# A recurrent megakernel: the fill turned by seven steps, gates of block 1 by DMA, low-rank products ahead of the base products

## The reference, cut to what matters

```python
# layer 0: shared MLP + 2 of 8 experts, gates from a sigmoid router
s = sigmoid(x_flat @ router_w.T + t_bias);  idx = top_k(s + router_bias, 2)
combine = sum(gates[:, :, None] * one_hot(idx, 8), axis=1)
H = gelu(einsum('nd,ehd->enh', x_flat, rw1));  O = einsum('enh,edh->end', H, rw2)
x = x + (silu(x @ sw1.T) * (x @ sw3.T) @ sw2.T + einsum('end,ne->nd', O, combine)) / 3
# layer 1: the sum and difference tree rebuilds v * gate
x = x + (x + x * sigmoid(silu(c @ W1.T + b1) @ W2.T + b2))
# layer 2: a1, b1, a2, b2 come from the condition (RANK = 8)
u = x a2;  mid = gelu(x @ base_down + u b2);  v = mid b1
x = x + (x + mid @ base_up.T + v a1)
# layer 3, for t in range(512):
Z = sigmoid(xz + H @ Whz.T + bhz);  R = sigmoid(xr + H @ Whr.T + bhr)
Ht = tanh(xh + (R * H) @ Whh.T + bhh);  H = Z * H + (1 - Z) * Ht;  Y = H @ Whq.T + bhq
x = x + Ys
```

## Time and profile before

| what | us |
|---|---|
| median of 3 runs (lowest, highest) | 1163.85 (1162.99, 1165.19) |
| the profiled execution, its own time | 1164.93 |
| its span | 1163.3 |
| TensorE busy | 1151.1 (99%) |
| VectorE busy | 893.1 (77%) |
| ScalarE busy | 509.4 (44%) |
| first scan of the state begins / last begins | 62.9 / 1157.9 |

### The profile page before, as it was taken

How to read it: one execution, slowest core, us unless ns; L and a number is a source line. 1 busy time by engine, 2 the same in 40 slices (tenths; PEclk the granted TensorE clock), 3 DMA queues, 4 the chain that set the end, 5 groups by cost and what they waited for, 6 DMA issues and landing times.

```text
span 1163.3 us, 56694 instructions
## 1 busy us (share of the span) xinstructions
PE 1151.1 (99%) x23581; PEld 1104.0 (95%) x23581; DVE 893.1 (77%) x5908; ACT 509.4 (44%) x2417; POOL 86.8 (7%) x163
## 2 busy tenths in 40 slices
PE   9899999999999999999999999999999999999998
PEld 8699999999999999999999999999999999999975
DVE  5568887777878777887777788777778777778765
ACT  1444444444444444444444444444444444444433
POOL 1200000000000000000000000000000000000000
PEclk9999999999999999999999999999999999999999
DMA  9511001111101110100111110011111001011000
GB/s 345 220 26 31 17 17 31 31 31 31 31 4 31 31 31 30 31 25 10 30 31 30 31 31 12 22 31 31 30 31 26 9 30 31 30 31 26 3 7 11
DMA packets 43297, 44.20 MB, mean 38 GB/s; under 512 B 7432, under 2 KB 39696, under 8 KB 41760
## 3 DMA queue, kind: packets, MB, share of 16 engines
q1 hardware_dynamic: 40720, 39.70, 11.3%
q10 hardware_dynamic: 2256, 0.82, 0.3%
q0 software_dynamic: 64, 0.07, 0.0%
HBM read 35.89 MB, written 4.69 MB: 35 GB/s over the span
## 4 chain that ended last, share of the span: by engine, by line
PE 96%; DVE 2%; DMA 1%; issue 1%; ACT 0%; SPq 0%; ACTq 0%; POOL 0%; DVEq 0%
PE bank L422 48%; PE gate_rh L422 28%; PE gate_z L422 12%; PE gate_rh L425 7%; DMA xt<-in_xT 1%; DVE state L1293 0%; ACT hin L885 0%; DVE peak L1367 0%; DVE upeaks L1364 0%; DVE upeaks L1375 0%; DVE upeaks L1373 0%; DVE hist L1295 0%; DVE state L1297 0%; DVE upeaks L1356 0%; DVE ge L1139 0%
## 5 line engine op out<-in xcount | busy, mean ns | idle before, releaser
L422 PE MATMUL gate_rh<-state,whp 128*128 128x8 f16 x5122 | 247.0, 166 | 0.0
L885 ACT ACTIVATE rg<-gate_rh 128x16 f32<-128x16 f32 x512 | 93.7, 183 | 337.7 <-PE gate_rh L422 337.7
L422 PEld LDWEIGHTS gate_rh<-state,whp 128*128 128x128 f16 x5122 | 199.3, 96 | 24.9 <-issue 8.0
L422 PE MATMUL bank<-x,upw 128*128 128x128 f16 x2880 | 218.3, 218 | 0.0
L422 PE MATMUL gate_rh<-rhp,whp 128*128 128x8 f16 x5120 | 216.6, 166 | 0.0
L539 PEld LDWEIGHTS <-whp 128*128 128x128 f16 x2046 | 201.6, 99 | 4.5
L422 PEld LDWEIGHTS gate_rh<-rhp,whp 128*128 128x128 f16 x5120 | 181.2, 96 | 7.4 <-issue 0.5
L885 ACT ACTIVATE zg<-zsum 128x16 f32<-128x16 f32 x512 | 110.6, 216 | 166.6 <-DVE zsum L1282 166.6
L422 PE MATMUL gate_z<-state,whp 128*128 128x16 f16 x4096 | 179.7, 176 | 0.0
L425 PE MATMUL gate_rh<-state,whp 128*128 128x8 f16 x1022 | 170.9, 167 | 1.8 <-DVE state L1293 0.6
L425 PE MATMUL gate_rh<-rhp,whp 128*128 128x8 f16 x1024 | 171.4, 167 | 0.3 <-DVE rhp L1277 0.3
(11 more groups left out here) (202 smaller groups left out, 1929.8 us busy)
## 6 DMA issues: line engine op xcount, KB each, us to landing
gates<-gates_t SPq DMA_DIRECT2D x30, 512.0 KB, 5.3
aw<-in_aw SPq DMA_DIRECT2D x4, 2048.0 KB, 23.3
out<-osb SPq DMA_DIRECT2D x32, 128.0 KB, 2.7
xt<-in_xT SPq DMA_DIRECT2D x30, 128.0 KB, 4.4
rw<-in_rw SPq DMA_DIRECT2D x2, 1024.0 KB, 10.2
sw<-in_sw SPq DMA_DIRECT2D x3, 512.0 KB, 6.7
wh<-in_wh SPq DMA_DIRECT2D x3, 256.0 KB, 11.8
wx<-in_wx SPq DMA_DIRECT2D x3, 256.0 KB, 20.0
```

The costliest lines, as they stand in the source:

```text
L422: return pe.matmul(o, w, x, start=start, stop=stop, skip_group_check=True)
L885: return act.activation(o, i, f, **kw)
```

## The change

The fill is turned by two more steps (TURN 5 to 7), so a fill round begins in real step 7 of its block, and must have its projections ready two fill steps sooner. For that the fill steps 4 to 10 are arranged anew: the low-rank product of g2 comes ahead of the base product of layer 2, `up_low` and `finish_l2` come a step sooner, the projections stand in fill steps 6 to 8 and not in 7 to 9, `sum_x` stands in step 7 and not in 8, the scores in step 6 (hole A) and not in 5 (hole B), `add_router_bias` in `early` of step 7 and not of 6, and the experts' gelu and gating one or two steps later. `exp_scores`, `fit_sum` and `fit_back` stay as they were.

In the set-up, the gates of block 1 go through DRAM on ScalarE's queue (a write of 16 KB, a broadcast read of 512 KB) and not through 8 calls on TensorE, the last experts of block 1 (4 chunks of 2 calls) move into the first two steps, `sum_x` for block 2 stands behind two of the chunks and reads its sum from the copy of x that was loaded early, the bits of two banks are set sooner, and each of the three wx loads has a semaphore of its own.

```diff
-TURN = 5
+TURN = 7
...
             def spread_gates(r):
-                sp.wait_ge(rows_ready, r - 1)
-                if r > 2:
-                    sp.wait_ge(gates_in, 16 * (r - 2))
+                sp.wait_ge(rows_ready, r)
+                sp.wait_ge(gates_in, 16 * (r - 1))
                 sp.dma_start(gates_dram, comb_rows[:]).then_inc(comb_out, 16)
-                sp.wait_ge(comb_out, 16 * (r - 1))
-                if r > 2:
-                    sp.wait_ge(ge47_done, r)
-                    sp.wait_ge(ge03_done, r)
+                sp.wait_ge(comb_out, 16 * r)
+                sp.wait_ge(ge47_done, r)
+                sp.wait_ge(ge03_done, r)
                 sp.dma_start(gates[:], gates_dram.rearrange("(q e) j -> q e j", q=QUADS)[:, 0:EXPERTS]
                              .partition_broadcast(P)).then_inc(gates_in, 16)
...
+            def experts_03_chunk(m, par, c):
+                if c == 0:
+                    pe.wait_ge(sa_done, count(m, 1))
+                    pe.wait_ge(xpow_done, 1)
+                up_chunks(A1, rw1, par, range(c, c + 1), ex03_done, c == 3)
+
             def between_z_h(m, par, s, has_y, has_l23, has_l0, has_router):
...
                 if has_y and s == 0:
                     y_products(later(m, -1), q, 0, 9)
                 if has_l0:
-                    for at, lo, hi in ((1, 11, 20), (7, 64, 73), (10, 77, 86)):
-                        if s == at:
-                            x_products(m2, par, lo, hi)
+                    if m[1] < 0 and s in (9, 10):
+                        experts_03_chunk(m2, par, 2 * (s - 9))
+                    if m[1] >= 0:
+                        for at, lo, hi in ((1, 11, 20), (9, 52, 61), (10, 75, 84)):
+                            if s == at:
+                                x_products(m2, par, lo, hi)
...
                     if s == 4:
-                        up_base(m1, (0,))
+                        pe.wait_ge(g2_done, count(m1, 1))
+                        low_in_rank(g2, start=True)
                     if s == 5:
-                        low_in_rank(g2, v_done)
-                    if s == 6:
-                        up_low(m1)
+                        pe.wait_ge(vm_done, count(m1, 1))
+                        up_base(m1, (1,))
+                    if s == 7:
+                        project_part(q, 3, 5)
                     if s == 8:
-                        project_part(q, 3, 5)
-                    if s == 9:
                         project_part(q, 8, 10)
-                if m[1] == BLOCKS - 2 and s in (1, 7, 10) or m[1] == BLOCKS - 2 and s > 10 or m[1] == BLOCKS - 1 and s > 0:
+                if has_router and s == 6:
+                    scores(later(m, 3), 1 - par).then_inc(scores_done, 1)
+                if m[1] == BLOCKS - 2 and (s in (1, 6) or s > 8) or m[1] == BLOCKS - 1 and s > 0:
                     keep_busy(2)
 
             def between_steps(m, par, s, has_y, has_l23, has_l0, has_router):
...
-                    for at, lo, hi in ((0, 0, 11), (1, 20, 24), (2, 24, 28), (3, 28, 42), (4, 42, 46), (5, 46, 50),
-                                       (6, 50, 64), (9, 73, 77), (10, 86, 96)):
-                        if s == at:
-                            x_products(m2, par, lo, hi)
+                    if m[1] < 0 and s in (9, 10):
+                        experts_03_chunk(m2, par, 2 * (s - 9) + 1)
+                    if m[1] >= 0:
+                        for at, lo, hi in ((0, 0, 11), (1, 20, 24), (2, 24, 28), (3, 28, 42), (4, 42, 46), (5, 46, 48),
+                                           (8, 48, 52), (9, 61, 75), (10, 84, 96)):
+                            if s == at:
+                                x_products(m2, par, lo, hi)
...
-                if has_router and s == 5:
-                    scores(later(m, 3), 1 - par)
                 if has_l23:
                     if s == 1:
                         mid_base(m1, (0,))
                     if s == 2:
-                        low_in_rank(x2, u_done)
+                        low_in_rank(x2).then_inc(u_done, 1)
                     if s == 4:
-                        up_base(m1, (1,))
-                    if s == 7:
+                        up_base(m1, (0,)).then_inc(v_done, 1)
+                    if s == 5:
+                        up_low(m1)
+                    if s == 6:
                         pe.wait_ge(x3_done, count(m1, 1))
                         pe.wait_ge(seeded, 2 * (m1[1] + 1))
                         project_part(q, 0, 3)
-                    if s == 8:
+                    if s == 7:
                         if has_router:
                             sum_x(later(m, 3))
                         project_part(q, 5, 8)
-                    if s == 9:
+                    if s == 8:
                         project_part(q, 10, 12)
...
-            sum_x((0, 2), 1)
             for k in range(KC):
                 i = mm(gate_rh[0][:, k * P:(k + 1) * P], low[:, 0, k * P:(k + 1) * P], ident[:], True, True)
             i.then_inc(lowT_pe, 1)
             pe.wait_ge(l2_in, 16)
             mid_base(m0)
+            pe.wait_ge(score_in, 3)
+            up_chunks(E47, rw1, 1, range(4, 5), ex47_done, False)
             pe.wait_ge(ready_dve, 4)
-            low_in_rank(x2, u_done)
-            spread(m1)
+            low_in_rank(x2).then_inc(u_done, 1)
+            set_bits(gate_rh[0]).then_inc(bits_set, 1)
+            up_chunks(E47, rw1, 1, range(5, 6), ex47_done, False)
+            pe.wait_ge(sa_done, 2)
+            sum_x((0, 2), 1)
             adapt(1, 0)
-            pe.wait_ge(score_in, 3)
-            up_chunks(E47, rw1, 1, range(4, 6), ex47_done, False)
+            up_chunks(E47, rw1, 1, range(6, 8), ex47_done, True)
             pe.wait_ge(low_dve, 2)
             mid_low(m0)
-            up_chunks(E47, rw1, 1, range(6, 8), ex47_done, True)
-            pe.wait_ge(xpow_done, 1)
-            set_bits(gate_rh[0]).then_inc(bits_set, 1)
+            adapt(1, 1)
             pe.wait_ge(g2_done, 1)
             pe.wait_ge(gs_done, 2)
             for k in range(KC):
                 i = mm(A3[:, 0:TOK], a2b1[:, k], g2[:, k], k == 0, k == KC - 1)
             i.then_inc(v_done, 1)
-            pe.wait_ge(sa_done, 2)
-            up_chunks(A1, rw1, 1, range(0, 2), ex03_done, False)
-            adapt(1, 1)
             pe.wait_ge(up_in, 16)
-            up_base(m0)
+            up_base(m0, start=True)
             first_reset_gate()
             pe.wait_ge(low_dve, 3)
             up_low(m0)
             set_bits(gate_z[0]).then_inc(bits_set, 1)
-            up_chunks(A1, rw1, 1, range(2, 4), ex03_done, True)
...
-                    if s == 8:
+                    if s == 10:
...
+            act.wait_ge(rows_ready, 1)
+            act.dma_start(gates_dram, comb_rows[:]).then_inc(comb_out, 16)
...
+            act.wait_ge(comb_out, 16)
+            act.dma_start(gates[:], gates_dram.rearrange("(q e) j -> q e j", q=QUADS)[:, 0:EXPERTS]
+                          .partition_broadcast(P)).then_inc(gates_in, 16)
-            sum_sizes((0, 2), 0)
+            act.wait_ge(ahead_in, 16)
+            sum_sizes((0, 2), xahead[:])
...
+                    if s == 5:
+                        keep_own(m1, vm, 1, v_done, vm_done)
                     if s == 6:
-                        keep_own(m1, vm, 1, v_done, vm_done)
-                    if s == 7:
                         finish_l2(m1, q)
...
-                        silu_a1_part(m2, s - 4)
+                    if s in (4, 7):
+                        silu_a1_part(m2, s // 7)
                     if s in (8, 9):
                         times_a3_part(m2, par, s - 8)
-                    if s in (10, 11):
-                        times_gate_part(m2, 1, s - 10, pe47_done, ge47_done)
-                if has_l0 and s in (12, 13):
-                    part = times_gate_part if m[1] >= 0 else times_spread_part
-                    part(m2, 0, s - 12, pe03_done, ge03_done)
+                if has_l0 and s in (11, 12):
+                    times_gate_part(m2, 1, s - 11, pe47_done, ge47_done)
+                if has_l0 and s in (13, 14):
+                    times_gate_part(m2, 0, s - 13, pe03_done, ge03_done)
                 if has_router:
-                    if s == 6:
-                        add_router_bias(m3)
-                    if s == 9:
-                        fit_x(m3)
-                    if s == 10:
-                        fit_x_end(m3)
-                    for at, k in ((11, 4), (14, 8), (14, 9), (15, 11), (15, 12)):
+                    if m[1] >= 0:
+                        if s == 7:
+                            add_router_bias(m3)
+                        if s == 9:
+                            fit_x(m3)
+                        if s == 10:
+                            fit_x_end(m3)
+                    for at, k in ((9, 1), (10, 3), (11, 5), (14, 9), (15, 11), (15, 12)):
                         if s == at:
                             gate_op(m3, k)
-                    if s == 14:
```

(60 more changed lines are left out.)

37 lines of the change are left out of this document (13 added, 24 removed).

## The result

Median over the runs that stood beside each other: 1163.42 us before, 1213.27 us after (1210.57 to 1218.68), a ratio of 1.043 with a 95% interval of 1.040 to 1.047. The forecast was 1197, its range ended at 1209. The profiled execution of the changed kernel took 1210.57 us, so the profile shows the cheapest of its runs; its span is 1208.8, which is 45.5 more than the 1163.3 before.

What follows compares the result with a forecast made beforehand. TensorE, without idle time in a step, was taken to bound the kernel; the time hung on the first scan and waits in the fill. -8.6 + 0 + 38.0 + 3.5 = +32.9 us gave 1197 us, range 1187 to 1209.

Steps and rivals of the forecast that it cites:

- the rival that had one: Each round's new TensorE wait also halves the clock afterwards: 51 us more, 1248 us; chance 6%.
- Part 3: Fill step 7: TensorE waits at `sum_x` for GpSimd's exponential and floor, 1.31 us a round, 38.0 us in 29 rounds.
- Part 1: Set-up: shorter wait, `spread`, experts and low clock bring the first scan 8.6 us sooner, bounds 5 and 10.5.
- some 0.4 of it hid x3: Set-up: of 1.8 us for block 1's last experts, some 0.4 hid x3, leaving 1.4 us gained.
- Part 2: Fill's turn and layer-2 order: covered by the recurrence's own matmuls, 0 us, bounds -1 and +3.
- Part 4: VectorE in fill step 15: `rest_x` makes `rhp` 0.12 us late a round, 3.5 us, bounds 0 and 7.
- The rival "no wait": Fill step 7: the sum reaches TensorE in time, so the set-up decides: 1159 us; chance 5%.

Runs made afterwards that it cites:

- e2: The changed kernel with five 512-column matmuls on zeros ahead of the waiting `sum_x` in fill step 7, so TensorE works through the wait; 1193.05 us.
- e1: The changed kernel with the floor of the sum issued ahead of the exponential in GpSimd's list of a round; 1158.23 us.
- e5: e1 with the first half of `rest_x` moved on VectorE from fill step 15 to step 0 of the next round; 1154.71 us.

## Why the prediction was wrong, step by step

- **The failed step: the clock set at nothing in the likeliest case.** The sum had no term for it; the rival that had one got 6%. It weighed one row, 4.12 us idle and then half rate, and called a stretch a third as long harmless because dense work stands on both sides. In fact 1.08 us was enough in half of the rounds: 17 us in the profiled execution, 20 between the medians of the changed kernel and e2. The rival was too high in its turn, 51 us: it took every round, where 15 of 29 were hit, and 1.75 us a stretch, where 1.1 to 1.2 came out. The rows of a low stretch show why it is less:

```profile
86.39 0.33 PE L422 MATMUL gate_rh<-state,whp 128*128 128x8 f16 x7
...
86.89 1.20 PE L422 MATMUL gate_rh<-x,wx 128*128 128x128 f32 x4
```

  Seven matmuls of 8 columns take 0.33 us there, and 0.32 at the full clock; four float32 matmuls of the projections take 1.20, while at the full clock 0.92 was enough for six. The fill slows, the recurrence hardly does.

  The section "HAM oscillation — how this bites in real kernels" of the Trainium skill (TensorE: Matmul & The Clock Gate) tells of a wait that recurs in every iteration and re-throttles the array each time. The page's waits are of 3 to 5 us each. Read as a rule for any recurring wait it gave this rival, and the trace agrees in part: 15 low stretches with 29 waits of 1.08 us, not one with each.
- **Part 3, the wait: right in its mechanism, 0.09 us a round too large.** `score` at +0.80 (156.80 - 156.00, predicted 0.80), exponential at +1.03 (1.03), floor at +2.67 (2.67). The hand-over to TensorE took 158.96 - 158.67 = 0.29 and not the 0.38 of the set-up, so TensorE went on at +2.96 instead of 3.05: 1.31 - 0.09 = 1.22 us a round, as measured, 35.4 for 38.0. The row of waits says only 1.08, since it counts from where TensorE ran dry; the difference between steps is the price.
- **Part 1, the set-up: right in kind; that the number is exact is luck.** First scan 54.3 predicted, 54.3 measured. But a head start of 1.2 us was there ahead of the change: the second half of the base product stood at 35.35 and not at 36.53. It goes with the clock at the very start, where the same 16 matmuls took 3.62 us before and 1.95 in this execution:

```profile
9.14 3.62 PE L422 MATMUL bank<-xt,sw 128*128 128x128 f32 x16
```

```profile
7.30 1.95 PE L422 MATMUL bank<-xt,sw 128*128 128x128 f32 x16
```

  In e2, whose set-up is that of the changed kernel, the second half stood at 36.77 and the first scan came at 54.9: without a head start the change's own part is 8.0 us, not 8.6. TensorE in the set-up of the changed kernel:

```profile
35.35 2.05 PE L422 MATMUL bank<-xt,sw 128*128 128x128 f32 x16
37.24 0.61 PE L422 MATMUL gate_rh<-ident,low 128*128 128x128 f32 x4
...
40.98 0.16 PE L422 MATMUL bank<-xsum,ones 128*128 128x1 bf16 x1 [0.69 <-POOL xsum L386]
...
45.23 1.93 PE L422 MATMUL gate_z<-aw,ah 128*32 128x256 f32 x32 [0.68 <-DMA aw<-in_aw]
...
50.09 1.13 PE L422 MATMUL gate_rh<-x,wx 128*128 128x128 f32 x8 [0.56 <-issue]
```

  The transposes no longer wait. `sum_x` waits 0.69 where I had put no wait: the floor ahead of it took 1.19 us and not the 0.23 that the sum took from the earlier trace rows (the last section shows why). aw2 holds up the second `adapt` for 0.68 (predicted 0.4). The 0.56 ahead of x3's projections is no new cost: a matmul on zeros stands there in the list, e1's trace has its record and 0.34 idle behind it, and the sum had about 0.4 for this ("some 0.4 of it hid x3").
- **Part 2, turn and layer-2 order: right.** e1 bounds it at 2.8 us together with step 15, which alone takes 2.0; in e5, where step 15 is relieved, the steps take 1093.7 us for 1095.0 before. Predicted 0 between -1 and +3.
- **Part 4, fill step 15: right in kind, half its size.** 0.07 us a round for 0.12; 2.0 us for 3.5. e5 removes it.
- **The rival "no wait"** gave 1159 us. It was wrong for this kernel, and e1, which makes it true by one swap, took 1158.2.

The range was narrower than its own parts: the upper bounds given for them add up to 44 - 5 + 3 + 7 = +49, or 1213, and not +45. A range up to 1213 would have come close to the measured time, but by terms that measured 35.4, 0 and 2.0; the clock, which did it, would still be missing.

The terms that were forecast, with their sizes as measured, give 1163.4 - 8.6 + 35.4 + 2.0 = 1192.2 us; e2, where only the clock is given back, took 1193.05.

## What to carry to other kernels

Where an engine's list puts a long operation ahead of a short one, ask who waits for the short one: here a floor of 0.23 us stood behind an exponential of 1.67 us that nobody needed yet, and one swap was worth 55 us. When a wait is put into every round of a TensorE-bound kernel, price it twice, once as itself and once for the clock, and don't put the second at nothing because the wait is short. Matmuls on zeros in the hole test that in one run: if the time falls although the step stays as long, the difference is the clock.
